# Two convolution layers: squares summed group by group, a second input buffer, and another order for the regrouping transfers

## The chip, the cores and the metric

The kernel runs on one core of a Trainium2 chip. The metric is device time in microseconds (us), lower is better; the time given is the median of several executions. The core has a matrix engine (TensorE, PE in the rows, with its weight loads PEld), a vector engine (VectorE, DVE), a scalar engine (ScalarE, ACT), GpSimd (POOL), and SyncE (SP), which here issues every DMA transfer. Each engine runs its own list of instructions in order, and semaphores order them against each other.

## The reference, cut to what matters

The input is 8 images of 32 channels and 256 x 256 points, float32. Four layers follow each other, each adding its result to its normalised input. The change touches only layer 0, two hyperbolic 3x3 convolutions:

```python
def _hconv(x, w, b):
    return _project(_expmap0(_conv3x3(_logmap0(x), w, b)))
...
out = _hconv(x, w1, b1)
out = _hbn(out, g1, beta1)
out = _hrelu(out)
out = _hconv(out, w2, b2)
```

`_logmap0` multiplies each point's 32 channels by a factor that depends on their norm, `_expmap0` and `_project` do the same to the result. So each point needs two sums of squares over the channels, one before and one after the convolution, and two factors that are then spread over the channels again.

## The kernel before

`conv_layer` is called twice, with `first=True` and `first=False`; I call the calls the first and the second layer. The 256 rows of the images are cut into 32 bands of 8 rows, and the 8 images into two halves of four; the 128 partitions hold 4 images x 32 channels. A loop of rounds runs over the bands, software-pipelined: in round n, band n is loaded and squared, band n-1 gets its input factors and is multiplied (`u`), band n-2 is convolved, band n-3 is multiplied by its output factors and stored. Each engine has its own `round_`, written out by hand, and the order of steps in it is the order of its work.

- **TensorE.** `convolve(r, h, groups)` makes 12 matmuls of 512 columns for each of 4 groups of a half, into two PSUM banks in turn (`conv[:, k % 2]`); `sum_squares(r)` sums the squares of the 20 input rows into `pc[:, 0]`; `sum_out(r, h)` those of the 8 output rows of a half into `pc[:, 1]`; `fill_u` and `fill_out` spread the factors into `spread` by 8, 8 and 4 or by 8 and 8 matmuls of 256 columns. The order in a round: convolve half 0 groups 0 and 1, `fill_out` 0, convolve groups 2 and 3, `fill_u` 0, convolve half 1 group 0, `fill_u` 1, group 1, `sum_squares`, `fill_u` 2, group 2, `sum_out` of half 0, `fill_out` 1, group 3, `sum_out` of half 1.
- **ScalarE.** `evacuate` copies each group out of PSUM with the bias (L456) and squares it into `sqv` (L457); `square` (L430) and `normalize` (L436) read the input tile `xt`; `logarithms` (L440, L441) only in the first layer. Both squares of band n come after all four evacuations of half 0.
- **VectorE.** `roots` (from L597) starts once `summed_out` and `summed_u` say that both sums are there, and makes the factors; `take_out` (L665) and `product_u` in `take_u` (L644) multiply; `measure` (L670) takes statistics. `take_out` of half 1 is the last step of a round.
- **SyncE.** In a round: the load of band n (three transfers for each half, L387 to L389), once band n-1 is squared and normalised, as `xt` is one buffer; the store of half 0 (L401); `regroup` of both halves, 16 transfers of 129 KB each (L396), which lay out four row-shifted copies of `u` in `uc` for the convolution; the store of half 1. `regroup(r, 0)` waits for `u_done`, given when all 10 rows of half 0 are multiplied, and `regroup(r, 1)` for the last piece of half 1 and the end of the convolution that reads `uc` of half 1 before.

Of the kernel before, what the change touches and what calls it, by code (L numbers as in the profile page):

```python
# [28 lines left out]
P = 128  # L29
QUAD = 32  # L30
# [284 lines left out]
def conv_layer(net, source, scale, bias, weights, conv_bias, target, stats, first):  # L315
# [6 lines left out]
    with ExitStack() as local:  # L322
        def sb(name, shape, dt=F32):
            return net.sb(local, name, shape, dt)
        xt = sb("xt", [P, HALVES, HALO, COLS])
# [5 lines left out]
        sqv = sb("sqv", [P, HALVES, TILE])  # L331
# [6 lines left out]
        nc_, l1, l2, sl, pl, xx, spread_of_u, spread_of_out = (sb(k, [P, COLS]) for k in (  # L338
            "nclip", "l1", "l2", "sl", "pl", "xx", "factor_u", "factor_out"))
# [6 lines left out]
        loaded, uc_loaded, measured = ([sem(f"{k}{h}") for h in range(2)] for k in ("loaded", "uc_loaded", "measured"))  # L346
        stored = [[sem(f"stored{parity}{h}") for h in range(2)] for parity in range(2)]
# [10 lines left out]
        def rounds(eng, round_):  # L358

            for n in range(4):  # L360
                round_(n, n % 2)
            with eng.Fori(2, BANDS // 2) as pair:
                for parity in range(2):
                    round_(pair * 2 + parity, parity)
            for n in range(BANDS, BANDS + 5):
                round_(n, n % 2)

        @block.sync
        def _(sp):
# [4 lines left out]
            def load(r):  # L374
                for h in range(HALVES):
                    wait_both(sp, normed, 2 * (r - 1) + h + 1, squared, 2 * (r - 1) + h + 1)
# [10 lines left out]
                    sp.dma_start(xt[:, h, 1:BAND + 1, :].rearrange("p r w -> p (r w)"), main).then_inc(loaded[h], 16)  # L387
                    sp.dma_start(xt[:, h, 0, :], above).then_inc(loaded[h], 16)
                    sp.dma_start(xt[:, h, BAND + 1, :], below).then_inc(loaded[h], 16)  # L389

            def regroup(r, h):
# [27 lines left out]
        def _(act):  # L419
# [3 lines left out]
            def source_of(h):  # L423
                return xt[:, h].rearrange("p r w -> p (r w)"), *(vec[:, h:h + 1] if first else vec for vec in (scale, bias))

            def square(r, h):
                src, scale_h, bias_h = source_of(h)
                wait_past(act, summed_u, 2 * (r - 1) + h + 1)
                act.wait_ge(loaded[h], 48 * r + 48)
                a.activation(sq[:, h, :], src, ACT.Square, bias=bias_h, scale=scale_h).then_inc(squared, 1)  # L430

            def normalize(r, h):
                src, scale_h, bias_h = source_of(h)
                wait_past(act, taken_u if h else u_done, 3 * r if h else r)
                act.wait_ge(loaded[h], 48 * r + 48)
                a.activation(xn[:, h, :], src, ACT.Identity if first else ACT.Relu, bias=bias_h, scale=scale_h).then_inc(normed, 1)  # L436

            def logarithms(r):
                act.wait_ge(normsq, r + 1)
                a.activation(l1[:], nc_[:], ACT.Ln, bias=1.0, scale=1.0)  # L440
                a.activation(l2[:], nc_[:], ACT.Ln, bias=1.0, scale=-1.0).then_inc(logs, 1)  # L441

            def evacuate(r, parity, h, groups):
                if groups[0] == 0:
# [3 lines left out]
                    wait_past(act, summed_out, 2 * (r - 1) + h + 1)  # L448
                for k in groups:
                    p, o = k // 2, k % 2  # L450
                    act.wait_ge(conv_ready, (2 * r + h) * 4 + k + 1)
                    src = conv[:, k % 2, :].rearrange("p (i w) -> p i w", i=2)
                    rows = slice(4 * p + o, 4 * p + o + 3, 2)
                    v_rows, sq_rows = (tile_.rearrange("p (r w) -> p r w", w=COLS)[:, rows, :]
                                       for tile_ in (v_sb[:, parity, h, :], sqv[:, h, :]))
# [26 lines left out]
        def _(pe):  # L482
# [14 lines left out]
            def sum_out(r, h):  # L497
                if h == 0:
                    wait_past(pe, read, r + 2)
                pe.wait_ge(evacuated, (2 * r + h + 1) * 4)  # L500
                for k in range(BAND):
                    b = BAND * h + k
                    q4 = QUAD * (b % 4)
                    last = m.matmul(pc[q4:q4 + QUAD, 1, :], c["ones"][:, b // 4, :], sqv[:, h, COLS * k:COLS * k + COLS],
# [1866 lines left out]
```

## Time and profile before

| what | us |
|---|---|
| median of 3 runs | 12041.97 (12029.0 to 12056.08) |
| profiled execution, its time | 12020.56 |
| profiled execution, its span | 12018.7 |
| TensorE busy in the span | 9492.6 (79%) |
| VectorE busy | 9408.9 (78%) |
| ScalarE busy | 8396.4 (70%) |

The busy shares are means over a program of several stages. The two convolution layers lie between about 250 and 2720 us of the span, about a fifth of it; the rest is not touched by the change. In that fifth the order of waits within one round matters, and the rows below show one round of each layer.

### The profile page before, as it was taken

How to read it: one execution, taken by the hardware profiler on the slowest of the kernel's cores; microseconds unless marked ns; L12 is line 12 of the kernel's file. 1: busy time of each engine (PE TensorE's matmuls, PEld its weight loads, DVE VectorE, ACT ScalarE, POOL GpSimd, SP SyncE). 2: the span in 40 equal slices, each digit the busy share in tenths (PEclk: the TensorE clock that was granted, in tenths of full speed). 3: DMA queues.
4: the chain of work that ended last, by engine and by line, in shares of the span. 5: the costliest groups of instructions: out<-in, count | busy, mean ns of one | idle time of the engine just before them, and what ended most of it. 6: DMA issues, size and time to landing. Idle time of an engine off the chain costs nothing. (4 is left out here: it accounts for less than half of the span.)

```text
span 12018.7 us, 360844 instructions
## 1 busy us (share of the span) xinstructions
PE 9492.6 (79%) x152226; PEld 4623.4 (38%) x152226; DVE 9408.9 (78%) x10971; ACT 8396.4 (70%) x5579; POOL 298.0 (2%) x132
## 2 busy tenths in 40 slices
PE   0888778885657799868888888888888888887787
PEld 0333223333435666533333333333333333333444
DVE  6677656657776666579999999999999999998776
ACT  0555455555531133279999999999999999998777
POOL 0000000000004500000000000000000000000000
PEclk9999999997879899989999999999999999998899
DMA  7888788886642244355555555555555555554555
GB/s 265 236 239 239 208 228 246 244 229 243 269 195 64 69 153 153 127 100 105 104 102 108 102 106 104 107 102 105 102 109 101 107 101 107 104 107 75 178 176 162
DMA packets 1165596, 1796.78 MB, mean 149 GB/s; under 512 B 124832, under 2 KB 929824, under 8 KB 1094048
## 3 DMA queue, kind: packets, MB, share of 16 engines
q1 hardware_dynamic: 1164320, 1777.49, 58.1%
q8 instruction: 1079, 17.68, 0.7%
q14 instruction: 197, 1.61, 0.1%
HBM read 701.15 MB, written 402.65 MB: 92 GB/s over the span
## 5 line engine op out<-in xcount | busy, mean ns | idle before, releaser
L1886 DVE SCALAR_TENSOR_TENSOR grown_ex<-ratio,ex 128x2048 f32<-128x2048 f32 x1024 | 2330.8, 2286 | 250.9 <-PE out L2019 107.4
L2019 PE MATMUL out<-ex,kan_basis 32*32 32x512 f32 x32768 | 1451.1, 654 | 637.8 <-DVE z L1868 359.6
L1764 ACT ACTIVATE ex<-ex 128x2048 f32<-128x2048 f32 x1024 | 1925.8, 1899 | 4.1
L2019 PE MATMUL out<-grown_ex,kan_basis 32*32 32x512 f32 x32768 | 1563.8, 645 | 51.7 <-DVE grown_ex L1886 50.8
L547 PE MATMUL conv<-uc,w 128*32 128x512 f32 x12288 | 1442.8, 611 | 21.0 <-DMA uc<-u 21.0
L1760 ACT ACTIVATE ex<-kin,offset 128x2048 f32<-128x2048 f32 x512 | 1013.2, 1991 | 68.8 <-PE out L2019 60.5
L456 ACT ACTIVATE v<-conv,cb 128x512 f32<-128x512 f32 x512 | 350.5, 684 | 789.8 <-PE conv L547 786.4
L2019 PEld LDWEIGHTS out<-ex,kan_basis 32*32 32x32 f32 x32768 | 396.6, 107 | 1113.5 <-issue 1045.1
L2019 PEld LDWEIGHTS out<-grown_ex,kan_basis 32*32 32x32 f32 x32768 | 541.3, 107 | 673.5 <-issue 582.4
L2138 DVE TENSOR_TENSOR d<-xt 128x2313 f32<-128x2313 f32 (+2 forms) x256 | 622.1, 2494 | 215.3 <-PE acc L2195 215.0
L2195 PE MATMUL acc<-d,weights 32*32 32x512 f32 x16384 | 667.1, 632 | 113.3 <-issue 109.6
L547 PEld LDWEIGHTS conv<-uc,w 128*32 128x32 f32 x12288 | 371.4, 112 | 881.1 <-issue 844.6
L644 DVE TENSOR_TENSOR u<-xn,spread 128x512 f32<-128x512 f32 (+2 forms) x320 | 379.3, 1218 | 377.9 <-PE spread L512 377.8
L2160 ACT ACTIVATE d<-d,steep 128x2313 f32<-128x2313 f32 (+2 forms) x256 | 534.0, 2159 | 35.7 <-DVE d L2138 35.7
L1246 ACT COPY tmp<-t_ps 128x512 f32<-128x512 f32 x256 | 149.9, 586 | 585.4 <-PE t_ps L1329 585.4
L430 ACT ACTIVATE sq<-xt,bias,scale 128x2560 f32<-128x2560 f32 x128 | 323.0, 2523 | 327.4 <-DMA xt<-t 186.3
L1760 ACT ACTIVATE ex<-z,offset 128x2048 f32<-128x2048 f32 x256 | 504.3, 1993 | 37.9 <-DVE z L1852 35.1
L1760 ACT ACTIVATE ex<-y,offset 128x2048 f32<-128x2048 f32 x256 | 509.1, 1989 | 0.0
L2195 PEld LDWEIGHTS acc<-d,weights 32*32 32x32 f32 x16384 | 364.9, 106 | 369.0 <-issue 281.3
L1971 PE MATMUL norm<-sq,c_kan_ones 128*32 128x128 f32 x10240 | 355.4, 279 | 190.4 <-DVE kin L1852 88.0
L1981 PE MATMUL norm<-rstd,c_sel 32*128 32x128 f32 x10240 | 381.8, 286 | 149.7 <-DVE q L1838 73.3
L1981 PEld LDWEIGHTS norm<-rstd,c_sel 32*128 32x128 f32 x10240 | 322.0, 189 | 426.8 <-DVE q L1838 237.7
(284 smaller groups left out, 17527.2 us busy)
## 6 DMA issues: line engine op xcount, KB each, us to landing
uc<-u SPq DMA_DIRECT2D x2048, 129.0 KB, 2.8
xt<-in_x SPq DMA_DIRECT2D x128, 1024.0 KB, 7.3
t<-v SPq DMA_DIRECT2D x128, 1024.0 KB, 5.8
back_k<-ku SPq DMA_DIRECT2D x1024, 128.0 KB
xt<-in_x SPq DMA_DIRECT2D x32, 2048.0 KB, 7.8
xt<-t SPq DMA_DIRECT2D x64, 1024.0 KB, 7.6
tt<-t SPq DMA_DIRECT2D x64, 1024.0 KB, 10.8
x<-x SPq DMA_DIRECT2D x64, 1024.0 KB, 4.9
```

The costliest lines, as they stand in the source:

```text
L456: a.activation(v_rows, src, ACT.Identity, bias=cb[:, 0:1])
L547: last = m.matmul(conv[QUAD * b:QUAD * b + QUAD, k % 2, :], w_sb[:, o, d, :], uc[:, h, b, 2 * p:2 * p + 2, d:d + COLS], start=(d == 0), st ...
L644: return v.tensor_tensor(inside(u[:, h, first_row:first_row + rows, 1:COLS + 1]), inside(xn[:, h, at].rearrange("p (r w) -> p r w", w=COLS ...
L1760: a.activation(ex[:, j], norm_out(kind, h), ACT.Square, bias=k["offset"][:, kind - 1, 2 * j:2 * j + 1]).then_inc(args, 1)
L1764: a.activation(ex[:, j], ex[:, j], ACT.Exp, scale=-1.0).then_inc(exps, 1)
L1886: v.scalar_tensor_tensor(grown_ex[:, j % 2], ratio[:], LARGEST, ex[:, j], ALU.min, ALU.mult).then_inc(grown, 1)
L1971: last = m.matmul(norm[rows(quarter), 0, 0:P], k["c_kan_ones"][:, 0 if kind in (K1, K2) else 1, i, :], sq[:, block_:block_ + P], start=(i ...
L1981: last = m.matmul(norm[:, quarter, P * i:P * i + P], k["c_sel4"][rows(quarter), i, :], y[rows(quarter), :], start=(i == 0), stop=(i == GRO ...
L2019: last = m.matmul(out[rows(i), g, :], k["kan_basis"][rows(g), kind - 1, n, :], base[rows(g), cols(i)], start=(n == 0), stop=(n == BASES - ...
L2138: v.tensor_tensor(d[:, h, n, rows, columns], there, xt[:, parity, h, rows, columns], ALU.subtract).then_inc(diff_ready, 1)
L2160: a.activation(t, t, ACT.Tanh, scale=steep[:, h:h + 1]).then_inc(tanh_ready, 1)
L2195: last = m.matmul(acc[quad(k), h, g, :], weights[quad(g), n, :], source_tile[quad(g), row + 2 * k:row + 2 * k + 2, column:column + COLS], ...
```

## The change

- `xt` has two buffers by the parity of the band; SyncE loads band n+1 in round n (band 0 ahead of the loop) and waits only for band n-1 to be squared and normalised. The steady loop of all engines ends a pair earlier.
- `regroup` takes a list of row shifts. Shifts 0 and 1, which need only the first eight rows of half 0, go out once the first product of `take_u` is done, shifts 2 and 3 after `u_done`. The wait on the convolution is that of half 0 before.
- SyncE issues the store of half 1 ahead of `regroup` of half 1.
- `sum_out` is cut by group: after each evacuation two matmuls instead of eight after four. `sqv` is a ring of four slots in place of two halves. TensorE's `sum_squares` moves up ahead of `fill_u` 0, and `fill_out` 1 up to stand right behind `fill_u` 2.
- ScalarE squares half 0 of band n after two evacuations, half 1 after a third; the other evacuations move by one place.
- Small VectorE tiles share memory (`nc_`, `xx`, `l1`, `l2`, `pl`, `sl`); the wait on `spread_u` moves ahead with that.

```diff
-        xt = sb("xt", [P, HALVES, HALO, COLS])
+        xt = sb("xt", [P, 2, HALVES, HALO, COLS])
-        sqv = sb("sqv", [P, HALVES, TILE])
+        sqv = sb("sqv", [P, 4, BANK])
...
-            def load(r):
+            def load(r, parity):
                 for h in range(HALVES):
-                    wait_both(sp, normed, 2 * (r - 1) + h + 1, squared, 2 * (r - 1) + h + 1)
+                    wait_both(sp, normed, 2 * (r - 2) + h + 1, squared, 2 * (r - 2) + h + 1)
...
-                wait_both(sp, taken_u if h else u_done, 3 * r + 3 if h else r + 1, conv_ready, (2 * (r - 1) + h + 1) * 4)
-                for b in range(GROUP):
-                    for k in range(4):
+                if h == 0:
+                    wait_both(sp, taken_u if some[0] == 0 else u_done, 3 * r + 1 if some[0] == 0 else r + 1, conv_ready, (2 * (r - 1) + 1) * 4)
+                else:
+                    wait_both(sp, taken_u, 3 * r + 3, conv_ready, (2 * (r - 1) + 2) * 4)
+                for k in some:
+                    for b in range(GROUP):
...
+            load(0, 0)
+
             def round_(n, parity):
-                if exists(n):
-                    load(n)
+                if exists(n + 1):
+                    load(n + 1, 1 - parity)
                 if exists(n - 3):
                     store(n - 3, 1 - parity, 0)
                 if exists(n - 1):
-                    regroup(n - 1, 0)
-                    regroup(n - 1, 1)
+                    regroup(n - 1, 0, (0, 1))
+                    regroup(n - 1, 0, (2, 3))
                 if exists(n - 3):
                     store(n - 3, 1 - parity, 1)
+                if exists(n - 1):
+                    regroup(n - 1, 1, (0, 1, 2, 3))
...
                 for k in groups:
                     p, o = k // 2, k % 2
+                    wait_past(act, summed_out, (2 * r + h) * 4 + k - 3)
...
                 if exists(n - 2):
                     evacuate(n - 2, parity, 0, (0, 1))
+                if exists(n):
+                    square(n, parity, 0)
                 if first and exists(n - 1):
                     logarithms(n - 1)
                 if exists(n - 2):
-                    evacuate(n - 2, parity, 0, (2, 3))
+                    evacuate(n - 2, parity, 0, (2,))
                 if exists(n):
-                    square(n, 0)
-                    square(n, 1)
+                    square(n, parity, 1)
                 if exists(n - 2):
-                    evacuate(n - 2, parity, 1, (0, 1))
+                    evacuate(n - 2, parity, 0, (3,))
+                    evacuate(n - 2, parity, 1, (0,))
                 if exists(n):
-                    normalize(n, 0)
+                    normalize(n, parity, 0)
                 if exists(n - 2):
-                    evacuate(n - 2, parity, 1, (2,))
+                    evacuate(n - 2, parity, 1, (1,))
                 if exists(n):
-                    normalize(n, 1)
+                    normalize(n, parity, 1)
                 if exists(n - 2):
-                    evacuate(n - 2, parity, 1, (3,))
+                    evacuate(n - 2, parity, 1, (2, 3))
...
-            def sum_out(r, h):
-                if h == 0:
+            def sum_out(r, h, k):
+                if h == 0 and k == 0:
                     wait_past(pe, read, r + 2)
-                pe.wait_ge(evacuated, (2 * r + h + 1) * 4)
-                for k in range(BAND):
-                    b = BAND * h + k
+                pe.wait_ge(evacuated, (2 * r + h) * 4 + k + 1)
+                for i in range(2):
+                    b = BAND * h + 4 * (k // 2) + k % 2 + 2 * i
...
                 if exists(n - 2):
-                    convolve(n - 2, 0, (0, 1))
+                    convolve(n - 2, 0, (0,))
+                    for k in (1, 2):
+                        convolve(n - 2, 0, (k,))
+                        sum_out(n - 2, 0, k - 1)
                 if exists(n - 3):
                     fill_out(n - 3, 0)
                 if exists(n - 2):
-                    convolve(n - 2, 0, (2, 3))
+                    convolve(n - 2, 0, (3,))
+                    sum_out(n - 2, 0, 2)
+                if exists(n):
+                    sum_squares(n)
                 if exists(n - 1):
                     fill_u(n - 1, 0)
                 if exists(n - 2):
                     convolve(n - 2, 1, (0,))
+                    sum_out(n - 2, 0, 3)
                 if exists(n - 1):
                     fill_u(n - 1, 1)
                 if exists(n - 2):
                     convolve(n - 2, 1, (1,))
-                if exists(n):
-                    sum_squares(n)
+                    sum_out(n - 2, 1, 0)
                 if exists(n - 1):
                     fill_u(n - 1, 2)
-                if exists(n - 2):
-                    convolve(n - 2, 1, (2,))
-                    sum_out(n - 2, 0)
                 if exists(n - 3):
                     fill_out(n - 3, 1)
                 if exists(n - 2):
+                    convolve(n - 2, 1, (2,))
+                    sum_out(n - 2, 1, 1)
                     convolve(n - 2, 1, (3,))
-                    sum_out(n - 2, 1)
+                    sum_out(n - 2, 1, 2)
+                    sum_out(n - 2, 1, 3)
```

## Rows read from the trace of the kernel before

**Rows 1.** Busy time by engine, a steady stretch of each layer; clock, DMA share, GB/s last

```profile
400.00:1400.00 1000.00, 856.84 (x8952) 306.65 (x8948) 717.91 (x1099) 546.41 (x587) 0.00 (x0) 0.95 0.85 240
1700.00:2600.00 900.00, 774.15 (x8272) 275.65 (x8264) 539.49 (x711) 488.48 (x494) 0.00 (x0) 0.99 0.89 245
```

**Rows 2.** Timeline of SyncE's queue: start, us, regroupings, first and last steady of each layer

```profile
306.78 22.65 SPq L396 DMA_DIRECT2D uc<-u  x32
...
1431.31 21.43 SPq L396 DMA_DIRECT2D uc<-u  x32
...
1565.52 23.22 SPq L396 DMA_DIRECT2D uc<-u  x32
...
2662.13 21.63 SPq L396 DMA_DIRECT2D uc<-u  x32
```

**Rows 3.** Timeline, one round of the first layer: start, us, work [idle before, releaser]

```profile
808.57 0.69 DVE L597 TENSOR_SCALAR q<-pc 128x512 f32<-128x512 f32 x1 [2.89 <-PE pc L504]
...
814.31 0.68 ACT L457 ACTIVATE sqv<-conv,cb 128x512 f32<-128x512 f32 x1
...
823.67 0.35 DVE L634 TENSOR_SCALAR factor_u<-sl,edge 128x256 f32<-128x256 f32 x1 [0.26 <-issue]
...
824.15 1.74 PE L512 MATMUL spread<-factor_u,c_sel 32*128 32x256 f32 x16 [2.31 <-DVE factor_u L634]
...
829.58 1.15 PE L512 MATMUL spread<-factor_u,c_sel 32*128 32x256 f32 x16
...
830.66 2.79 PE L547 MATMUL conv<-uc,w 128*32 128x512 f32 x24
...
833.27 2.33 PE L493 MATMUL pc<-sq,c_ones 128*32 128x256 f32 x40
...
835.53 0.71 PE L512 MATMUL spread<-factor_u,c_sel 32*128 32x256 f32 x8
...
838.78 1.04 PE L504 MATMUL pc<-sqv,c_ones 128*32 128x256 f32 x16
...
839.75 1.15 PE L512 MATMUL spread<-factor_out,c_sel 32*128 32x256 f32 x16
...
840.83 2.79 PE L547 MATMUL conv<-uc,w 128*32 128x512 f32 x24
...
845.01 1.07 PE L504 MATMUL pc<-sqv,c_ones 128*32 128x256 f32 x16 [1.39 <-ACT sqv L457]
...
846.15 0.69 DVE L597 TENSOR_SCALAR q<-pc 128x512 f32<-128x512 f32 x1 [2.89 <-PE pc L504]
```

**Rows 4.** Same round, VectorE's products and statistics, and the second logarithm

```profile
816.32 0.40 ACT L441 ACTIVATE l<-nclip 128x256 f32<-128x256 f32 x1
...
826.13 2.29 DVE L644 TENSOR_TENSOR u<-xn,spread 128x2048 f32<-128x2048 f32 x1 [0.91 <-PE spread L512]
...
830.79 2.42 DVE L644 TENSOR_TENSOR u<-xn,spread 128x512 f32<-128x512 f32 x3 [0.80 <-PE spread L512]
...
833.13 1.28 DVE L670 BATCH_NORM_STATS2 part<-v 128x6 f32<-128x512 f32 x2
...
836.31 1.22 DVE L644 TENSOR_TENSOR u<-xn,spread 128x1024 f32<-128x1024 f32 x1 [1.91 <-PE spread L512]
```

**Rows 5.** Busy time by stretch, 4 us of the same round, columns as in rows 1

```profile
824.00:828.00 4.00, 3.85 (x28) 1.58 (x32) 3.09 (x4) 1.26 (x1) 0.00 (x0) 0.57 1.04 335
```

**Rows 6.** Timeline, the second layer: a load's issue, both squares, and their sum

```profile
2024.87 0.36 SPq L387 DMA_DIRECT2D xt<-t  x1
...
2034.58 2.52 ACT L430 ACTIVATE sq<-xt,bias,scale 128x2560 f32<-128x2560 f32 x1 [4.01 <-DMA xt<-t]
...
2038.00 2.52 ACT L430 ACTIVATE sq<-xt,bias,scale 128x2560 f32<-128x2560 f32 x1 [0.89 <-DMA xt<-t]
...
2040.57 1.49 PE L493 MATMUL pc<-sq,c_ones 128*32 128x256 f32 x20 [1.92 <-ACT sq L430]
```

**Rows 7.** DMA issues of the whole run: KB each, median us to landing

```profile
uc<-u SPq DMA_DIRECT2D x2048, 129.0 KB, 2.8
```

More of the change, by code:

```diff
@@ L337, in conv_layer @@
         q, rn, t_, a_ = (sb(k, [P, 2, COLS]) for k in ("q", "rn", "t", "a"))
-        nc_, l1, l2, sl, pl, xx, spread_of_u, spread_of_out = (sb(k, [P, COLS]) for k in (
-            "nclip", "l1", "l2", "sl", "pl", "xx", "factor_u", "factor_out"))
+        spread_of_u, spread_of_out = (sb(k, [P, COLS]) for k in ("factor_u", "factor_out"))
+        nc_, xx, l1, l2, pl, sl = t_[:, 0], t_[:, 1], a_[:, 0], a_[:, 1], q[:, 1], spread_of_u
         pc = net.ps(local, "pc", [P, 2, BANK])[:, :, 0:COLS]
@@ L345, in sem @@
             return net.sem(local, name)
-        loaded, uc_loaded, measured = ([sem(f"{k}{h}") for h in range(2)] for k in ("loaded", "uc_loaded", "measured"))
-        stored = [[sem(f"stored{parity}{h}") for h in range(2)] for parity in range(2)]
+        uc_loaded, measured = ([sem(f"{k}{h}") for h in range(2)] for k in ("uc_loaded", "measured"))
+        loaded, stored = ([[sem(f"{k}{parity}{h}") for h in range(2)] for parity in range(2)] for k in ("loaded", "stored"))
         ready = sem("params")
@@ L361, in rounds @@
                 round_(n, n % 2)
-            with eng.Fori(2, BANDS // 2) as pair:
+            with eng.Fori(2, BANDS // 2 - 1) as pair:
                 for parity in range(2):
                     round_(pair * 2 + parity, parity)
-            for n in range(BANDS, BANDS + 5):
+            for n in range(BANDS - 2, BANDS + 5):
                 round_(n, n % 2)
@@ L386, in load, with regroup @@
                         below = source[(r + 1) % BANDS, h, :, 0:COLS]
[L387 to L391, printed above, removed]
-                wait_both(sp, taken_u if h else u_done, 3 * r + 3 if h else r + 1, conv_ready, (2 * (r - 1) + h + 1) * 4)
-                for b in range(GROUP):
-                    for k in range(4):
+                    sp.dma_start(xt[:, parity, h, 1:BAND + 1, :].rearrange("p r w -> p (r w)"), main).then_inc(loaded[parity][h], 16)
+                    sp.dma_start(xt[:, parity, h, 0, :], above).then_inc(loaded[parity][h], 16)
+                    sp.dma_start(xt[:, parity, h, BAND + 1, :], below).then_inc(loaded[parity][h], 16)
+            def regroup(r, h, some):
+                if h == 0:
[4 more added lines that the diff above has]
+                    for b in range(GROUP):
                         sp.dma_start(uc[QUAD * k:QUAD * k + QUAD, h, b, :, :],
@@ L421, in _, with source_of, square, normalize @@
             act.wait_ge(ready, 48)
[L423 to L427, printed above, removed]
+            def source_of(parity, h):
+                return xt[:, parity, h].rearrange("p r w -> p (r w)"), *(vec[:, h:h + 1] if first else vec for vec in (scale, bias))
+            def square(r, parity, h):
+                src, scale_h, bias_h = source_of(parity, h)
                 wait_past(act, summed_u, 2 * (r - 1) + h + 1)
-                act.wait_ge(loaded[h], 48 * r + 48)
+                act.wait_ge(loaded[parity][h], 24 * (r - parity) + 48)
                 a.activation(sq[:, h, :], src, ACT.Square, bias=bias_h, scale=scale_h).then_inc(squared, 1)
-            def normalize(r, h):
-                src, scale_h, bias_h = source_of(h)
+            def normalize(r, parity, h):
+                src, scale_h, bias_h = source_of(parity, h)
                 wait_past(act, taken_u if h else u_done, 3 * r if h else r)
-                act.wait_ge(loaded[h], 48 * r + 48)
+                act.wait_ge(loaded[parity][h], 24 * (r - parity) + 48)
                 a.activation(xn[:, h, :], src, ACT.Identity if first else ACT.Relu, bias=bias_h, scale=scale_h).then_inc(normed, 1)
@@ L453, in evacuate @@
                     rows = slice(4 * p + o, 4 * p + o + 3, 2)
-                    v_rows, sq_rows = (tile_.rearrange("p (r w) -> p r w", w=COLS)[:, rows, :]
-                                       for tile_ in (v_sb[:, parity, h, :], sqv[:, h, :]))
+                    v_rows = v_sb[:, parity, h, :].rearrange("p (r w) -> p r w", w=COLS)[:, rows, :]
+                    sq_rows = sqv[:, k, :].rearrange("p (i w) -> p i w", i=2)
                     a.activation(v_rows, src, ACT.Identity, bias=cb[:, 0:1])
@@ L595, in roots @@
                 if with_out:
[L596 removed]
+                    dve.wait_ge(summed_out, 8 * ro + 8)
                 v.tensor_scalar(q[:, both], pc[:, both], EPS_NORM * EPS_NORM, None, ALU.max).then_inc(read, 1)
@@ L621, in factors_u @@
                 if first:
+                    wait_past(dve, spread_u, 3 * r)
                     dve.wait_ge(logs, r + 1)
-                    v.tensor_tensor(sl[:], l1[:], l2[:], ALU.subtract)
+                    v.tensor_tensor(sl[:], l1, l2, ALU.subtract)
                     v.drain()
@@ L626, in factors_u @@
                     v.drain()
-                    v.scalar_tensor_tensor(pl[:], pl[:], 1.0, sl[:], ALU.add, ALU.subtract)
+                    v.scalar_tensor_tensor(pl, pl, 1.0, sl[:], ALU.add, ALU.subtract)
                     v.drain()
-                    v.scalar_tensor_tensor(pl[:], q[:, 0], 0.04, pl[:], ALU.is_lt, ALU.mult)
+                    v.scalar_tensor_tensor(pl, q[:, 0], 0.04, pl, ALU.is_lt, ALU.mult)
                     v.drain()
-                    v.tensor_tensor(sl[:], sl[:], pl[:], ALU.add)
+                    v.tensor_tensor(sl[:], sl[:], pl, ALU.add)
                     v.drain()
-                wait_past(dve, spread_u, 3 * r)
                 v.tensor_scalar(spread_of_u[:], sl[:], edge[:, bass.ds(r, 1)], None, ALU.mult).then_inc(factors_u_ready, 1)
```

21 lines of the change are left out of this document (10 added, 11 removed).

## Prediction

> **What bounds the kernel now.** I read the busy shares of the page first: no engine is full, and the shares mix stages, so they decide nothing. The view by stretch then gives each layer alone. In the steady part of the first layer TensorE is busy 86% of the time at a mean clock of 0.95 and the DMA engines 85%; in the second 86%, 0.99 and 89% [rows 1]. Neither is full, but the DMA share is what a shorter round can run into. The timeline of SyncE's queue gives the period of a round: 30 rounds from 306.78 to 1431.31 are 37.48 us each, 30 from 1565.52 to 2662.13 are 36.55 us [rows 2]. A change of a round by 1 us is thus worth about 62 us (31 steady rounds in each of two layers).
>
> The timeline of one round shows the ring of waits that makes 37.48. Call Q the moment at which VectorE starts `roots` (808.57). From Q it works alone until the input factor is ready at 824.02, and TensorE, which has run out of convolutions, is idle for the last 2.31 us of that. It starts `fill_u` 0 at 824.15, 15.58 after Q. From there TensorE is the path: `fill_u` 0 and a convolution group 5.43, `fill_u` 1 1.08, a group 2.61, `sum_squares` 2.26, `fill_u` 2 and a group 3.25, `sum_out` of half 0 0.97, `fill_out` 1.08, the last group with its evacuation 4.18 (1.39 of it idle), `sum_out` of half 1 until the next Q 1.14 [rows 3]. The sum is 15.58 + 22.00 = 37.58, the distance to the next Q at 846.15. So work that TensorE does after the factor counts in full, and work that it does before it is free as long as it fits into VectorE's 15.58.
>
> The 5.43 is also too long: `fill_u` 1 and the group behind it take 1.08 + 2.61 = 3.69. The granted clock in 824 to 828 is 0.57 [rows 5], so most of that stretch ran at 1.2 in place of 2.4 GHz, right after the 2.31 us of idle. It costs 5.43 - 3.69 = 1.74 us a round, in the first layer only; in the second the mean clock is 0.99 [rows 1].
>
> In the second layer the ring is another one. The logarithms are absent, the factor comes early, but the squares wait for their input: a load issued at 2024.87 lets the first square start at 2034.58, the second, with its own load behind, at 2038.00, and TensorE stands 1.92 us before the second half of the sum [rows 6]. The load itself is issued late, because `xt` has one buffer and the load stands in SyncE's queue behind 32 regrouping transfers of about 0.70 us each (22.65 for 32, [rows 2]).
>
> **The change on TensorE, first layer.** I walk the new round from Q, with the steps of rows 3 at full clock: a group 2.60, a fill of eight 1.08, a fill of four 0.65, `sum_squares` 2.26.
>
> A `sum_out` is now a pair of matmuls. Eight in a row take 0.97, thus 0.24 a pair if pairs pack as well; but a pair uses two of the four column strips of the array, while the row of eight uses each strip twice. If a strip is what limits, eight are two turns of each strip, and a pair is one whole turn: 0.97 / 2 = 0.48. So 0.24 to 0.48; I take 0.44, near the upper end, as the next convolution matmul goes to strip 0 in order. The Trainium skill, "TensorEngine Tiling (Array Packing)", Key Properties, says that tiles operate independently and can load and multiply in parallel; by that a pair on two of four strips wastes the others, which is the upper end, and the lower end would make each round about 0.8 us shorter on the path. The trace of before has no pair alone, so no row decides.
>
> Ahead of the factor TensorE now has, from Q - 0.2: groups 0 and 1, pair, group 2, pair, `fill_out` 0, group 3, pair, `sum_squares`: 4 x 2.60 + 3 x 0.44 + 1.08 + 2.26 = 15.06, done at Q + 14.86. That is inside 15.58, so the 2.26 of `sum_squares` and three pairs cost nothing there; the cover is VectorE's chain, and it has 0.7 us left. Do the squares come in time? ScalarE ends its second evacuation at Q + 6.42 [rows 3]; then a square 2.52 [rows 6], two logarithms of 0.4 [rows 4], an evacuation of about 1.25, a square 2.52: Q + 13.6, half way through `sum_squares` (it starts at 12.6 with half 0). Yes.
>
> VectorE's chain keeps its 15.58: `take_out` in it needs `fill_out` 0, done at Q + 9.6, before about Q + 10.1 when it is needed. The moved wait on `spread_u` was met a round earlier, and the shared tiles add no instruction: nothing.
>
> After the factor: `fill_u` 0 1.08, a group 2.60, a pair 0.44, so `fill_u` 1 starts at 19.70. Then comes a new wait. `fill_out` 1 stood behind a convolution and a `sum_out`; now it follows `fill_u` 2 at once and needs VectorE to have taken the last piece of `u`. VectorE needs 1.21 from the start of `fill_u` 1 to the product, 2.34, statistics 1.28, the last product 1.22 [rows 4]: 6.05, about 6.1 with the signal, while TensorE has only 1.08 + 2.60 + 0.44 + 0.65 = 4.77 to do. So it stands 1.3 us, and the two last groups and pairs are queued behind it. `fill_out` 1 starts at 25.8. Then 1.08, a group 2.60, a pair 0.44, the last group and its evacuation 4.18, and the last pair with the signal about 0.5 (in place of 1.14): the next Q is at 34.6.
>
> So a first-layer round goes from 37.48 to 34.6. In parts: `sum_squares` off the path -2.26, full clock -1.74, `sum_out` of half 0 -0.97 and of half 1 -0.64, three pairs +1.32, the wait for `take_u` +1.3: -3.0. The clock is my choice: the 2.31 us of idle ahead of the drop shrink to 0.7.
>
> **The second layer.** With two buffers the load has a round more, and the waits of rows 6 go. Then nothing stops TensorE before `fill_u` 0 except its own order: it gets there at Q + 14.86 (squares at 12.7, factor at about 12). The rest is as above, 34.6 - 15.58 = 19.0: a round of 33.9.
>
> **SyncE and the transfers.** `regroup` 1 still waits for the last group of half 1, which ends 1.9 before Q. The store put ahead of it waits for `take_out` 1, some 2.5 us earlier: hidden. 16 transfers at 0.70 go out until Q + 9.4, and half 1 lands at about Q + 11.5 (2.8 to landing, [rows 7]), against Q + 15.9 when it is first read. Then six loads and the store of half 0. `regroup` 0 can start at taken_u, Q + 14.86 + 1.21 + 2.29 = Q + 18.4 in the second layer (19.1 in the first), goes on past `u_done` without a stop, and lands 11.2 - 0.7 + 2.8 = 13.3 later: Q + 31.7, against Q + 33.7 when the next round reads it. Margin 2.0. Begun at `u_done` (Q + 18.97 + 1.21 + 0.68 = 20.9), as before, it would land at 34.2 and miss by 0.5.
>
> The backlog takes from this margin. Two loads of 1.28 MB and a store of 1 MB, 3.56 MB at 335 GB/s [rows 5], need 10.6 us; issued from Q + 9.4 with their latency they fill the engines until about Q + 22, so the first regroupings start about 2 us late. In the regrouping the engines have little to spare, so half of it may stay: margin about 1 to 0. The Trainium skill, "DMA: Bandwidth & Descriptors", HWDGE ordering, says that on each engine descriptors are consumed in ring order; it speaks against the early load, since every byte of it is ahead of the regrouping. Nothing in the trace contradicts that. Over a round the DMA work is 0.85 x 37.48 = 31.9 and 0.89 x 36.55 = 32.5 us [rows 1, 2]; at 34.6 and 33.9 that is 92% and 96%. I add 0.3 to the second layer for it: 34.2.
>
> **The sum.** 31 x (37.48 - 34.6) = 89 and 31 x (36.55 - 34.2) = 73: 162 us. The head of each layer, where band 1 loads early, may give up to 10 more; I take none. The profiled time 12020.6 becomes 11859; the median shown is 21 us above it, so 12042 - 162 = 11880.
>
> **Rivals.**
> - *The clock falls all the same* in the first layer: against it, idle of 1.9 us in the second layer goes with a mean clock of 0.99 [rows 1, 6]; for it, the new 1.3 us wait is followed by the last evacuation's 1.4. +1.74 x 31 = 54: 11934.
> - *The DMA engines set the round.* If the backlog stays whole and mixed traffic is dearer, both rounds are about 36: 31 x (1.5 + 0.55) = 64 saved, 11978. For it: the shares of 92 and 96%. Against: 31.9 and 32.5 us of work leave 2 us.
> - *Pairs are cheap and the head gains:* 0.6 less each round and 10 us: 11830.
> - *Slower: late regrouping of half 0.* Same place, `uc` of half 0. If the loads and the store hold the engines until Q + 25.5 (13.1 us from issue to the second square in rows 6, and the store behind) and regrouping then keeps its 0.70 pace, it lands at about Q + 38.3; the round is then 38.5, above both old periods: 31 x (1.0 + 1.95) = 92, so 12134. In the second layer it costs more than the change gives there from a landing 4.7 us later than I reckon (36.4 in place of 31.7).
> - *Nothing moves:* a ring that I did not see keeps 37 us a round; 12042.
>
> **Chances.** Forecast 0.58 (11850 to 11915), clock 0.10, DMA 0.13, cheap pairs 0.06, nothing 0.05, slower 0.08. Faster by over 0.2% (24 us, about what a measurement of this kernel can tell) 0.87, within it 0.05, slower 0.08. The range goes from the cheap pairs to just past the DMA case: 11820 to 11985.
>
> **What would show it.** The period between starts of `q<-pc` at 34.6 and 34.2; clock 1.0 in the first layer; a wait of 1.3 us of `spread<-factor_out` on the product of `u`; no wait of a square on its load; pairs every 0.44. The forecast is wrong if convolution groups wait for `uc` for more than a few tenths each round, or if the clock still drops.

## The result and the profile after

The changed kernel takes 11747.68 us (median of 4, 11732.55 to 11756.04) against 12043.52 us before, a ratio of 0.9753 with a 95% interval of 0.9736 to 0.977. It is 296 us faster. The forecast was 162 us, 11880, with 11820 as the lower end: right in sign, wrong in size. One execution of the kernel before, made beside the last set of runs, took 15765.76 us at a granted clock of 0.629 and is left out of every number here.

The steady stretches of both convolution layers of the changed kernel, by stretch as in [rows 1] (the length, busy us of TensorE, its weight loads, VectorE, ScalarE and GpSimd, then clock, DMA share and GB/s):

```profile
300.00:1300.00 1000.00, 900.34 (x9636) 384.34 (x9632) 757.86 (x1156) 576.60 (x630) 0.00 (x0) 1.00 0.91 254
1500.00:2400.00 900.00, 828.00 (x8890) 345.92 (x8884) 578.80 (x762) 519.75 (x533) 0.00 (x0) 1.00 1.02 262
```

TensorE is busy 90% and 92% in place of 86%, its clock is 1.00 in both, and the DMA share has risen to 0.91 and 1.02. Rounds are 34.87 and 33.97 us, from VectorE's timeline, two starts of `roots` 24 rounds apart in each layer:

```profile
387.90 0.69 DVE L612 TENSOR_SCALAR q<-pc 128x512 f32<-128x512 f32 x1 [5.20 <-PE pc L513]
...
1224.86 0.69 DVE L612 TENSOR_SCALAR q<-pc 128x512 f32<-128x512 f32 x1 [5.21 <-PE pc L513]
...
1573.05 0.69 DVE L612 TENSOR_SCALAR q<-pc 128x512 f32<-128x512 f32 x1 [5.20 <-PE pc L513]
...
2388.35 0.69 DVE L612 TENSOR_SCALAR q<-pc 128x512 f32<-128x512 f32 x1 [5.20 <-PE pc L513]
```

The forecast had 34.6 and 34.2. So the rounds of the convolution layers came close to the forecast, and the missing part is elsewhere. The first and last start of one instruction in each later stage show where. First the kernel before, then the changed one (instructions by tile: duration ns min/median/max, first and last start):

```profile
L756 SPq DMA_DIRECT2D tt<-t x64: 327/350/1031, 2737.7 to 3437.3; - x64
...
L1683 SPq DMA_DIRECT2D kin<-y x512: 543/674/1830, 5139.2 to 10919.5; - x171
...
L1764 ACT ACTIVATE ex<-ex x1024: 1889/1897/1918, 5177.7 to 11109.9; 128x2048 f32<-128x2048 f32 x171
...
L2166 ACT ACTIVATE ot<-acc,half x64: 1947/1967/1974, 11172.4 to 12009.7; 128x2048 f32<-128x2048 f32 x64
```

```profile
L772 SPq DMA_DIRECT2D tt<-t x64: 328/362/1014, 2584.8 to 3283.6; - x64
...
L1699 SPq DMA_DIRECT2D kin<-y x512: 543/680/1683, 4995.0 to 10701.0; - x171
...
L1780 ACT ACTIVATE ex<-ex x1024: 1887/1896/1921, 5033.7 to 10890.8; 128x2048 f32<-128x2048 f32 x171
...
L2182 ACT ACTIVATE ot<-acc,half x64: 1943/1967/1973, 10953.1 to 11745.3; 128x2048 f32<-128x2048 f32 x64
```

`tt` is first loaded when the convolution layers are over: 2737.7 against 2584.8, 153 us earlier. From the first `kin` to the last `ex` is the window layer (layer 2): 5970.7 against 5895.8, 75 us shorter. From there to the last `ot` is the pattern layer (layer 3): 899.8 against 854.5, 45 us. No line of these two is touched by the change. The stages between, with the last microseconds, lost 9. The profiled spans differ by 264 us: 153 + 75 + 45 - 9.

One round of the first layer after, as in [rows 3 and 4]:

```profile
806.40 0.69 DVE L612 TENSOR_SCALAR q<-pc 128x512 f32<-128x512 f32 x1 [5.20 <-PE pc L513]
...
821.79 1.15 PE L521 MATMUL spread<-factor_u,c_sel 32*128 32x256 f32 x16 [0.83 <-DVE factor_u L650]
...
825.48 0.61 PE L513 MATMUL pc<-sqv,c_ones 128*32 128x256 f32 x4
...
826.02 1.15 PE L521 MATMUL spread<-factor_u,c_sel 32*128 32x256 f32 x16
...
830.24 0.71 PE L521 MATMUL spread<-factor_u,c_sel 32*128 32x256 f32 x8
831.02 1.22 DVE L660 TENSOR_TENSOR u<-xn,spread 128x1024 f32<-128x1024 f32 x1 [0.17 <-PE spread L521]
...
832.30 1.15 PE L521 MATMUL spread<-factor_out,c_sel 32*128 32x256 f32 x16 [1.34 <-DVE u L660]
833.37 3.20 PE L556 MATMUL conv<-uc,w 128*32 128x512 f32 x25
...
840.54 0.63 PE L513 MATMUL pc<-sqv,c_ones 128*32 128x256 f32 x4 [1.36 <-ACT sqv L464]
...
841.22 0.69 DVE L612 TENSOR_SCALAR q<-pc 128x512 f32<-128x512 f32 x1 [5.20 <-PE pc L513]
```

From Q: 15.39 to `fill_u` 0 (idle 0.83 in place of 2.31), 4.23 to `fill_u` 1, 6.28 to `fill_out` 1 with a new wait of 1.34, 1.07, and 7.85 to the next Q: 34.82. A pair of matmuls takes 0.54 (825.48 to 826.02).

### The profile page after: what moved, and what is told of

Its sections match the earlier page's. It is cut to its first block and busy times, and to the rows that moved or that the text cites. A ratio compares the mean times of both kernels' runs of the same rounds, so it can differ in the third digit from the quotient of the medians.

```text
span 11754.3 us, 361509 instructions
## 1 busy us (share of the span) xinstructions
PE 9447.6 (80%) x152226; PEld 4753.9 (40%) x152226; DVE 9406.4 (80%) x10971; ACT 8384.4 (71%) x5579; POOL 298.1 (3%) x132
## 5 line engine op out<-in xcount | busy, mean ns | idle before, releaser
L556 PEld LDWEIGHTS conv<-uc,w 128*32 128x32 f32 x12288 | 460.0, 109 | 756.3 <-issue 649.0
L2031 PE MATMUL out<-ku,kan_silu 128*128 128x512 f32 x1024 | 473.6, 605 | 0.3 <-issue 0.3
```

Source lines behind the costliest of these rows:

```text
L556: last = m.matmul(conv[QUAD * b:QUAD * b + QUAD, k % 2, :], w_sb[:, o, d, :], uc[:, h, b, 2 * p:2 * p + 2, d:d + COLS], start=(d == 0), st ...
L2031: m.matmul(out[:, i, :], k["kan_silu"][:, kind - 1, :], silu_of(kind, h)[:, cols(i)], start=False, stop=False)
```

## The experiments

In the table are the lengths of stages in each profile: convolution layers from the first `roots` to the first load of `tt`, window and pattern layers as above. Apart from the start, ahead of the first `roots`, the other stages sum to the same within 14 us in all builds. The kernel before was measured again beside each set of runs: 12038.73 beside before_pad, after_pad, fillout_late and regroup_whole, 12041.78 beside before_dve, after_dve, sums_late and one_buffer, 12031.0 beside before_both, after_both, fillout_first and the changed kernel again.

| kernel | median us | convolution | window | pattern |
|---|---|---|---|---|
| before | 12043.52 | 2479.5 | 5970.7 | 899.8 |
| before_pad | 11963.34 | 2478.6 | 5957.0 | 834.0 |
| before_dve | 11943.87 | 2476.2 | 5904.5 | 905.6 |
| before_both | 11908.25 | 2478.4 | 5892.0 | 842.7 |
| changed | 11747.68 | 2329.6 | 5895.8 | 854.5 |
| changed, again | 11740.42 | 2326.8 | 5882.2 | 866.1 |
| after_pad | 11784.73 | 2328.7 | 5900.5 | 883.4 |
| after_dve | 11803.97 | 2327.2 | 5964.6 | 845.0 |
| after_both | 11872.5 | 2328.2 | 5977.2 | 892.8 |
| regroup_whole | 11753.79 | 2353.6 | 5885.7 | 838.1 |
| sums_late | 11842.18 | 2446.6 | 5875.7 | 846.9 |
| one_buffer | 12299.04 | 2892.0 | 5899.4 | 851.0 |
| fillout_late | 11690.26 | 2296.3 | 5875.4 | 844.4 |
| fillout_first | 11700.81 | 2293.7 | 5882.4 | 851.9 |

### Where TensorE's code lies

What led to it are gaps of TensorE in the pattern layer that are put down to nothing but issue. The kernel before, then the changed one, TensorE's timeline:

```profile
11563.23 1.90 PE L2195 MATMUL acc<-d,weights 32*32 32x512 f32 x40 [0.47 <-issue]
...
11568.30 4.51 PE L2195 MATMUL acc<-d,weights 32*32 32x512 f32 x127 [0.47 <-issue]
11575.25 4.86 PE L2195 MATMUL acc<-d,weights 32*32 32x512 f32 x80 [2.44 <-issue]
11582.05 1.15 PE L2195 MATMUL acc<-xt,weights 32*32 32x512 f32 x32 [1.94 <-issue]
```

```profile
11382.52 4.49 PE L2211 MATMUL acc<-d,weights 32*32 32x512 f32 x127 [0.46 <-issue]
11388.38 2.32 PE L2211 MATMUL acc<-d,weights 32*32 32x512 f32 x61 [1.37 <-issue]
11394.31 1.35 PE L2211 MATMUL acc<-xt,weights 32*32 32x512 f32 x32 [3.61 <-issue]
```

Gaps of 0.5 to 3.6 us stand there, in the two kernels at other places of the same loop. From one to the next are 126 (11563.23 to 11568.30, by the lines left out between) or 127 matmul records, each with its weight load, where the gaps follow in the plainest way; others are 80 and 61 apart. The Trainium skill, "Runtime: NRT & Kernel Launch", Instruction fetch mechanics, says that code is refilled in blocks of 256 instructions and that a taken branch to a block that is no longer held waits for it. The distance of 126 or 127 pairs agrees with such a block, that of 80 and 61 is left unexplained. The changed kernel has some 2780 more TensorE instructions ahead of this loop, which is not a multiple of 256: its steady loop ends a pair of rounds earlier, so two more rounds of 168 matmuls are written out in each layer, and a matmul shows as two records with a weight load each, thus four instructions (2688 in all; the figure with the rest is a count of the code, not of a trace). So I moved the code and nothing else.

```diff
         def _(pe):
             pe.wait_ge(loaded, 16)
+            for _ in range(pads):
+                nc.tensor.matmul(pm[:, 1, 0:n], matrix[:], matrix[:, 0:n], start=True, stop=True)
             pe.wait_ge(own, 1)
```

before_pad has 54 of them, 216 instructions, in the first call alone. Expected:

> The kernel before with 54 tiny extra matmuls of TensorE at its start, where it idles over 200 us for the input statistics: 216 more instructions in its stream, none in a stage that is timed. The question is why the stages behind the convolutions, untouched by the change, became 110 us shorter. Theory A, placement: TensorE's code comes in blocks of 256 instructions (its gaps lie 127 or 128 matmuls apart), and what matters is where the loops of later stages lie in those blocks; the padding puts them where the changed kernel has them (to one instruction). Then the stages behind the convolutions become 90 to 130 us shorter, the pattern layer goes from 863 to about 819 us, the total to about 11930; the convolution rounds stay at 37.5 and 36.55 us. Theory B, the change carries over into later stages in another way (memory addresses, DMA queue, clock state): nothing moves, 12040.

Measured: the pattern layer goes from 899.8 to 834.0, the convolution layers stay, the window layer hardly moves, and the start costs 16 us. The median is 75 us lower, less than the 90 to 130 of theory A. The other way round, 10 matmuls in the changed kernel:

> The changed kernel with 10 tiny matmuls at its start: 40 instructions, which put TensorE's later loops where the kernel before has them in the blocks of 256 (to two instructions). Theory A, placement: the stages behind the convolutions lose what they had gained, 90 to 130 us, total 11840 to 11880, the pattern layer back to about 863 us; convolution rounds still 34.9 and 34.0 us. Theory B: 11748.

The pattern layer goes from 854.5 to 883.4 and the total up by 37, again less than expected. Both move the way of theory A in the pattern layer; the window layer is not explained by it.

### Where VectorE's code lies

The second code queue of the page (3: packets, MB, share) has fewer packets in every build of the changed kernel. Before, and changed:

```profile
q14 instruction: 197, 1.61, 0.1%
```

```profile
q14 instruction: 61, 0.50, 0.0%
```

By stretches, 154 of the 197 fall between 5400 and 11110 us, in the window layer, and 15 of the 61 in the same stretch of the changed kernel (5250 to 10950). In the view of waits over 5000 us of that layer (total, times, longest), ScalarE waits over and over for VectorE, before and changed:

```profile
ACT ratio L1769 <- DVE grown_ex L1886: 166.1, 54, 5.9
```

```profile
ACT ratio L1785 <- DVE grown_ex L1902: 44.6, 55, 3.7
```

That is 3.1 against 0.8 us a time, 121 us less in all, of which 52 come back as longer waits for TensorE (`ex` on `out`, 51.0 before, 103.1 changed). So VectorE's stream was shifted as well, by 110 instructions in before_dve (the loop shown) and by 20 in after_dve:

```diff
+            for _ in range(55):
+                v.memset(part[:, 0, 0:1], 0.0)
+                v.drain()
             pipeline(dve, BANDS // span, [(0, measure)])
```

> The kernel before with 110 small instructions of VectorE (memsets of one column, each with a drain) at its very start. Moving TensorE's code changed the pattern layer (900 to 834 us) but hardly the window layer (5971 to 5957), which is 75 us shorter in every build of the changed kernel; there the packets of code in the second code queue also are 61 instead of 197. Theory A: VectorE's loop of the window layer, some 352 instructions, straddles one block of code too many in the kernel before and is fetched anew in each pass; shifted by 110 it does not. Then the second code queue shows about 60 packets, the window layer is 55 to 80 us shorter (about 5900), less up to 10 us at the start: total about 11975. Theory B: another engine's code, or not code at all: 197 packets, window layer 5971, total about 12045.

> The changed kernel with 20 small instructions of VectorE at its start, which put its later loops where the kernel before has them, modulo 256. Theory A: about 190 packets of code in the second code queue, the window layer 55 to 80 us longer (about 5960), total 11810. Theory B: 61 packets, 11748.

The queue's line, the kernel before with 110 instructions more, and the changed one with 20 more:

```profile
q14 instruction: 58, 0.48, 0.0%
```

```profile
q14 instruction: 201, 1.65, 0.1%
```

The window layer goes to 5904.5 (-66) and 5964.6 (+69), the pattern layer stays within 10. ScalarE's wait follows: 44.9 us in all in the shifted kernel before, 166.4 in the shifted changed one. Theory A holds in both directions. In the median the memsets, which compute nothing, gain 98 us; between the two profiled executions it is 69. The 110 instructions do not put VectorE's code where the changed kernel has it: if 20 more in the changed kernel restore the place of before, modulo 256, the changed kernel is shifted by 236. They put it at another place at which the loop is not fetched anew.

> The kernel before with both paddings, TensorE's 54 matmuls and VectorE's 110 instructions at the start. Theory A (the place of the code of both engines makes the 110 us behind the convolutions, and each padding acts on its own stage): convolution layers as before (2479 us), window layer about 5900, pattern layer 834 to 855, 15 us lost at the start: total about 11885. What is then left to the changed kernel, 11748, is what the convolution layers gained, 150 us less 15. Theory B (the two do not add up): 11930 or more.

> The changed kernel with both paddings (TensorE 10 matmuls, VectorE 20 instructions), which put both engines' later loops where the kernel before has them. Theory A: window layer about 5965, pattern layer 880 to 900, convolution layers 2329 as changed: total 11845, 153 to 196 us below the kernel before. Theory B: 11800 or less.

Both together: the window layer 5892.0 and 5977.2, the pattern layer 842.7 and 892.8. The sum of the two layers moves by 136 us in the one (6870.5 to 6734.7) and by 120 in the other (6750.3 to 6870.0). In the medians the kernel before gains 123 with both (12031.0 to 11908.25), and the changed one loses 132 against its own repeat below (11740.42) or 125 against the first measurement. That the two paddings simply add up is shown only roughly: one by one they gain 75 and 98 in the kernel before, 173 where both together give 123, and lose 37 and 56 in the changed one, 93 where both together cost 125 to 132. The total is the firmer number. With both loops at their good places, the change itself is worth 11908.25 - 11740.42 = 168 us, of which some 18 are the paddings' cost at the start (the first `roots` at 275.8 in place of 258.2), thus 150; with the code where the kernel before has it, 12031.0 - 11872.5 = 159. The convolution stage says 150.

> The changed kernel once more, unchanged, to see how far the stages of a profile differ from one execution to the next. Theory A: stages repeat within 3 us, so differences of 10 to 20 us in the window and pattern layers between builds with the same place of code have a cause. Theory B: those two stages vary by 10 to 20 us from execution to execution, and only differences of 40 us and more count.

The convolution layers repeat within 3 us, the window and pattern layers differ by 14 and 12, in opposite directions. Theory B: in these two stages only differences well above that are read here. The place of the code passes that test over all 14 profiles: the window layer takes 5875.4 to 5904.5 us in the ten with few packets of VectorE's code and 5957.0 to 5977.2 in the four with many; the pattern layer takes 834.0 to 866.1 in the ten with TensorE's code at the changed kernel's place and 883.4 to 905.6 in the four with it at that of the kernel before.

### The order of TensorE, and what holds the second layer

```diff
-                if exists(n - 3):
-                    fill_out(n - 3, 1)
                 if exists(n - 2):
                     convolve(n - 2, 1, (2,))
                     sum_out(n - 2, 1, 1)
+                if exists(n - 3):
+                    fill_out(n - 3, 1)
+                if exists(n - 2):
                     convolve(n - 2, 1, (3,))
```

> The changed kernel with fill_out 1 put behind group 2 of half 1 again, so that it no longer follows fill_u 2 at once. TensorE's wait of 1.34 us on VectorE's last product should go. Theory A, TensorE's chain is the bound in both layers: rounds of 33.5 in the first and 32.7 in the second layer, 31 x 2.7 = 83 us less, 11665. Theory B, the DMA engines bound the second layer (share 1.02 in its steady part): the first layer gains 1.3 a round, the second 0 to 0.3: 11700. The instruction count is that of the changed kernel, so the later stages should stay.

First layer 33.61 a round, 1.26 less: the wait of 1.34 is gone. Second layer 34.10 on average, no better. Three starts of `roots` there, then the convolution between the first two:

```profile
2012.67 0.69 DVE L613 TENSOR_SCALAR q<-pc 128x512 f32<-128x512 f32 x1 [2.42 <-PE pc L513]
...
2048.52 0.69 DVE L613 TENSOR_SCALAR q<-pc 128x512 f32<-128x512 f32 x1 [2.42 <-PE pc L513]
...
2081.30 0.69 DVE L613 TENSOR_SCALAR q<-pc 128x512 f32<-128x512 f32 x1 [2.42 <-PE pc L513]
```

```profile
2014.03 2.79 PE L556 MATMUL conv<-uc,w 128*32 128x512 f32 x12 [1.40 <-DMA uc<-u]
```

Rounds of 35.85 and 32.78 take turns. In the long one the convolution waits 1.40 for the regrouping, 13 times in 800 us, and the clock over that round (2000 to 2035) is 0.95. Theory B fits the second layer: it stays at about 34 us when TensorE's list gets shorter, and what it waits for is the regrouping. That the rate of the DMA engines is the limit is not shown. The first layer of the same run keeps 33.61 a round at a DMA share of 1.03 (300 to 1300), so a share of about 1 is no wall by itself, and that the regroupings start too late or stand behind other transfers remains a rival that no run separates. The median transfer of `uc` lands after 3.9 us, 3.3 in the changed kernel and 2.8 before [rows 7], but fillout_first below, without long rounds, has 3.8.

> The changed kernel with fill_out 1 behind group 2 in the first layer only. The first layer should run 33.6 us a round as in the run with fill_out late in both, the second 34.0 as changed, without the alternation of 32.8 and 35.7. Convolution layers 2329 - 38 = 2291; total 11748 - 38 = 11710 if later stages stay as in the changed kernel, 11685 if they come out as in the run with fill_out late. Rival: the first layer's faster rounds were part of one whole with the second and nothing but noise differs: 2296.

Rounds of 33.62 and 33.96, no turns: the order of one layer can be chosen without the other. Convolution layers 2293.7, the shortest of all, by 2.6 us from fillout_late; the medians, 11700.81 and 11690.26, lie apart by no more than the window and pattern layers vary. They are 0.4% and 0.5% below the changed kernel.

```diff
                     sum_out(n - 2, 0, 2)
-                if exists(n):
-                    sum_squares(n)
...
                     sum_out(n - 2, 1, 0)
+                if exists(n):
+                    sum_squares(n)
                 if exists(n - 1):
                     fill_u(n - 1, 2)
```

> The changed kernel with sum_squares back ahead of fill_u 2. Same instruction count. In the first layer TensorE is then out of work 2.26 us earlier before the factor (0.83 + 2.26 = 3.1 us idle), and 2.26 more lie behind it, of which 1.34 fill the wait for the last product: +0.9 a round, 35.8. Theory A on the clock, a gap of over 2.3 us ahead of fill_u 0 brings half the clock for some 4 us as in the kernel before: +1.7 more, 37.5. Theory B: the clock stays up, 35.8. Second layer: TensorE gets to fill_u 0 earlier by 2.26 and pays 0.9: 32.7 by its own chain, but 33.7 or more if the DMA engines are the wall, as the run with fill_out late has it (34.2 on average). Total with A: 11748 + 31 x (2.6 - 0.2) = 11822; with B 11775.

First layer 39.26 a round, above both theories, in turns of 39.8 and 38.7; second 33.97, unchanged. The stretch right behind the gap ahead of `fill_u` 0, and the gap (timeline of the same kernel):

```profile
803.57 2.09 PE L521 MATMUL spread<-factor_u,c_sel 32*128 32x256 f32 x16 [3.07 <-DVE factor_u L650]
805.59 4.68 PE L556 MATMUL conv<-uc,w 128*32 128x512 f32 x24
...
819.07 1.15 PE L521 MATMUL spread<-factor_out,c_sel 32*128 32x256 f32 x16 [1.34 <-DVE u L660]
```

```profile
803.00:807.00 4.00, 3.43 (x24) 1.62 (x28) 2.63 (x4) 0.00 (x0) 0.00 (x0) 0.50 1.03 317
```

After 3.07 us of idle the granted clock is 0.50, 1.2 GHz, and `fill_u` 0 to `fill_u` 1 takes 7.06 (803.57 to 810.63) in place of 4.23: 2.83 lost. With the 2.26 of `sum_squares` it makes 5.1 a round. The round shown, one of 39.8, is 5.0 longer than in the changed kernel; the mean is 4.4, and what the shorter rounds save was not followed. I had credited the sum with filling the 1.34 wait, but that wait stays (819.07): it is `fill_u` 2, then the product that reads it, then `fill_out` 1, whatever stands ahead. In the second layer TensorE does not wait for the factor, its own list closes the ring, and moving work within the list changes nothing. My 32.7 there was wrong reasoning, and no evidence on the DMA engines.

### The buffers and the transfers

one_buffer loads band n at the start of round n into one `xt`:

```diff
-                if exists(n + 1):
-                    load(n + 1, 1 - parity)
+                if exists(n):
+                    load(n, parity)
```

> The changed kernel with one input buffer, the load of band n at the start of round n as before, everything else as changed. The load goes out after regroup of half 1, 9.4 us after Q, and the squares can start at about 19 and 22.5 after Q; ScalarE has them ahead of the third evacuation, so evacuations, convolutions and sum_squares stand until then, and fill_u 0 comes at about 26 in place of 15. Theory A (the new order depends on the second buffer): rounds of 40 us or more in both layers, total 12050 to 12400. Theory B (the buffer is worth only the waits that the profile of the kernel before shows in the second layer, 2 to 3 us a round): total 11830.

Rounds of 42.4 to 44.5 in the first layer; in the median 255 us more than the kernel before. Late in the first layer a square waits 8.17 us for its load, with the evacuations queued behind it on ScalarE:

```profile
1262.06 2.52 ACT L435 ACTIVATE sq<-xt,bias,scale 128x2560 f32<-128x2560 f32 x1 [8.17 <-DMA xt<-in_x]
```

The new order needs the second buffer; of its 20 KB in each partition, `sqv` gives 8 (16 before, 8 now) and the six shared small tiles 6.

regroup_whole sends all 16 transfers of half 0 at `u_done`:

```diff
-                    wait_both(sp, taken_u if some[0] == 0 else u_done, 3 * r + 1 if some[0] == 0 else r + 1, conv_ready, (2 * (r - 1) + 1) * 4)
+                    wait_both(sp, u_done, r + 1, conv_ready, (2 * (r - 1) + 1) * 4)
...
-                    regroup(n - 1, 0, (0, 1))
-                    regroup(n - 1, 0, (2, 3))
+                    regroup(n - 1, 0, (0, 1, 2, 3))
```

> The changed kernel with regroup of half 0 whole again, begun at u_done, some 2.4 us later. The profile of the changed kernel has the last transfer of half 0 landing about 2.5 us before the convolution reads it in the first layer and about 1.6 in the second. Theory A, those margins hold: first layer unchanged, second +0.8 a round, +25 us, 11773. Theory B, the split buys nothing: 11748 within 10. Theory C, transfers queue up behind the later start: both rounds +1 or more, 11810 or more.

Convolution layers 2353.6, +24: the steady first layer is unchanged at 34.9, the second averages 34.2, with single rounds up to 36.5 among 34.1, and much of the rest is in the first rounds of each layer (43.38 and 39.16 in place of 40.05 and 34.63 in the first, 42.18 and 38.02 in place of 39.46 and 34.31 in the second). The total moves by 6, since the later stages came out 26 us shorter in this profile. The 25 us expected are the 24 of the convolution stage in number alone: theory A had 0.8 a steady round of the second layer, and 0.2 came. The split is worth about 24 us, much of it while the rounds fill.

## Why the prediction was right or wrong

**The step that failed** is the sum: it took 31 rounds of each layer and held all else fixed, so the stages behind the convolutions stood in it at nothing, without a reason. Of 296 us, about 150 are the convolution layers, where 162 were forecast, and most of the rest comes from code that was moved, not changed: putting both engines' later loops back costs 125 to 132 us (after_both). No term and no rival had it, and the range reached only to cheap pairs. A clue was there: the code queues are on the page of the kernel before.

A smaller step of the same sum is the count of rounds. The steady round gained 2.61 in the first layer (forecast 2.88) and 2.58 in the second (forecast 2.35). That these two errors cancel is luck. By 31 each they give 161; from the first to the last `roots` each layer gained only 75 (1212.8 to 1137.9 and 1180.2 to 1104.9), as fewer than 31 rounds are steady.

**First layer.** 34.6 forecast, 34.87 measured. VectorE's chain 15.58, measured 15.39. The clock stays up, as chosen: the idle ahead of the factor is 0.83. sums_late shows the other branch: 3.07 us of idle bring 0.50. The wait of 1.3 us in front of `fill_out` 1 came as 1.34, with another cause than given: I had the statistics of VectorE in the way, but VectorE stands idle for 0.17 ahead of the last product, until `fill_u` 2 is there; the two paths are nearly equally long, and sums_late, where the wait stays at 1.34, bears out the second. A pair costs 0.54 in place of 0.44, beyond the bound of 0.48 that I had worked out. Both ends of that bound came from eight in a row, and left out what it may cost to change between kinds of matmul; that this is the cause is not shown.

**Second layer.** 34.2 forecast, 33.97 measured. The walk alone gives 33.9. The 0.3 added for the backlog was not needed: no wait for `uc` shows in the steady rounds. The margin is thin all the same. Taking 1.3 us off TensorE in this layer gives nothing, and regrouping begun at `u_done`, said to miss by 0.5, cost 0.2 a steady round. The Trainium skill, "DMA: Bandwidth & Descriptors", HWDGE ordering, says that on each engine descriptors are consumed in ring order, which spoke against the early load. The landing of `uc` did rise from 2.8 to 3.3, without reaching the path; that the ring order is why, no run here shows.

**The rivals.** The clock rival, the slower one, cheap pairs and "nothing moves" did not come. The DMA rival, rounds of 36, did not come either; its place, the regrouping, is what the second layer waits for once TensorE's list is shorter, at about 34.

**Open:** that the pattern layer is shorter with the code in one place than in another is shown only as an effect of place; which block is fetched when was not followed. What keeps the second layer at 34 is not separated into the rate of the transfers and their order. The 9 us lost between the stages lie within what builds with the same code there show (2405.5 to 2419.2 us for everything but the start and the three stages).

## What to carry to other kernels

Take the stages apart before crediting a change: here nearly half of the gain came from loops it does not touch. The place of a long loop in an engine's stream of instructions can be a parameter of its own, and a few dozen idle instructions at the start test it: one run to move the old kernel's code, one to move the new kernel's back. In a ring of waits across engines, work moved ahead of the wait that closes it is free only up to the idle time there, and a gap left there costs clock as well.

## What the runs showed of the hardware

- VectorE's loop of the window layer, the same instructions, was fetched anew again and again or hardly at all, by a shift of 20 instructions: 201 or 61 packets of code in the whole run, 66 to 75 us of 5900 in that layer.
- The place of TensorE's code moved the pattern layer from 899.8 to 834.0 us in the kernel before and from 854.5 to 883.4 in the changed one, 7% and 3%.
- Idle of 0.83 us ahead of `fill_u` 0 left the mean clock at 1.00. After 2.31 and 3.07 us of idle the granted clock was 0.57 and 0.50 over 4 us (0.50 is 1.2 GHz), at a loss of 1.74 and 2.83 us.
- A pair of 256-column matmuls on two of four column strips takes 0.54 us (one such pair read), eight on all four 0.97.
